# Second normalised rows split by tile and turned by a transposing DMA in the layers of a graph network kernel

## The chip, the cores and the metric

The kernel runs on one core of a Trainium2 chip. The metric is the device time of one execution in microseconds (us), lower is better. Five engines run their own instruction streams and meet only at semaphores: TensorE (PE in the rows), VectorE (DVE), ScalarE (ACT), GpSimd (POOL) and SyncE (SP, which here only issues DMAs). A DMA that SyncE or ScalarE issues stands in the rows as SPq or ACTq.

## The reference

The input is 6250 rows of 512 floats and 100000 edges sorted by destination. One block of a graph transformer is computed:

```
xn = layernorm(x)
x  = x + gnn(xn, src, dst) + linear_attention(xn)
x  = x + mixture_of_experts(layernorm(x))

gnn:  agg = segment_sum(xn[src], dst);  xn @ W1.T + b1 + (agg / deg) @ W2.T + b2
attention: q, k = relu(..), v;  vk = v'k over all rows;  q @ vk, divided by its last column; @ proj.T
experts: scores -> softmax over rows -> pooled row -> gate; best 2 of 8 experts on all rows, gelu twice
```

The rows of the second layernorm are called x2 after the sum and xn2 once normalised. Each expert matmul needs xn2 with features on the partitions, which is why xn2 is turned (transposed) tile by tile.

## The kernel before

**Tiles and stages.** The rows are T = 49 tiles of 128. Stage one normalises the rows, splits each float into a high and a low half in float16 (together near float32), stores them to a table in HBM and turns each tile into `xT[:, t]` (128 partitions x 8 x 128 float16: four high chunks, four low ones). Of the tiles from 21 on, two in three are turned by a transposing DMA from SyncE (18 in all), the others by TensorE. Then come the key products ("the K stage") and a short middle part.

**The layers.** `layer(i)`, i = 1 to 48, runs on every engine in a hand-written order. In layer i TensorE does the query matmuls of tile SEQ[i], turns the mean and the attention row of SEQ[i-1] (`turn_ah`, `turn_p`), multiplies (`own`, `gathered`, `mixed`), adds up neighbour rows for a tile ahead (`add_units`), and as its last work turns xn2 of SEQ[i-2] (`turn_x2`, four float32 transposes into a PSUM bank). SEQ is the order of the tiles, 0 to 37 first; tiles 47 and 48 (LATE) come between and their second half is done after the rest.

**Where the turned rows go.** At the start of layer i ScalarE copies the bank of tile SEQ[i-3] as the high half to `xT` (`x2T_high`), and VectorE subtracts it from the bank for the low half (`x2T_low`). Their place in the queues of ScalarE and VectorE matters: on ScalarE `x2T_high` stands right behind `keep_ah`, which ends the layer before, and ahead of `deviation`, `ahT_high` and `pT_high`; on VectorE `x2T_low` stands ahead of `statistics`, `ahT_low`, `pT_low`, `normal` and the rest. `gathered` on TensorE waits for `ahT_low` of the same layer.

**The gathers.** GpSimd issues 782 indirect DMAs (line 811), one each 128 rows of the table, four to a step. A ring of 16 slots holds four steps, so the gathers of step n+4 may not be issued before TensorE has added step n (`add_step`, line 928). The first is issued in the K stage, the last near the end of the layers. Three steps or so fall in a layer; a table computed at build time (`PLAN`) fixes where in TensorE's queue each is added.

**Spills.** The mean of a tile is made ahead of its use. For tiles below SPILLED = 25 it is written to HBM after `keep_ah` (`spill`, SyncE) and read back later (`fetch`, SyncE). In the loop over the layers SyncE does in this order:

```
if t not in LATE and t + WRITE < SPILLED:
    fetch(t + WRITE)
if AHEAD[i] is not None and AHEAD[i] < SPILLED:
    spill(AHEAD[i])
```

`spill(AHEAD[i])` waits for `keep_ah`, the last thing that ScalarE does in layer i. By the tables of the kernel the layers with a spill are i = 1, 2, 3, 5, 6, 7, 9, 10, 11, 13, 14, 15, 17, 18 and 19.

Of the kernel before, what the change touches and what calls it, by code (L numbers as in the profile page):

```python
# [16 lines left out]
ALU = mybir.AluOpType  # L17
ACT = mybir.ActivationFunctionType
# [3 lines left out]
N, D, E = 6250, 512, 100000  # L22
# [4 lines left out]
T = (N + P - 1) // P  # L27
# [52 lines left out]
def after(eng, sem, count):  # L80

    if not isinstance(count, int) or count > 0:
        eng.wait_ge(sem, count)
# [14 lines left out]
LATE = (T - 2, T - 1)  # L98
SEQ = [*range(38), LATE[0], *range(38, 42), LATE[1], *range(42, T - 2)]
K_AT, K_STEP, M_PARTS, LAYER, GATHERS, LANDING, ADDING, UNITING = 5.0, 5.75, (7.5, 3.5, 8.0), 11.9, 5.02, 5.0, 0.55, 1.6  # L100
TURN = {t: i for i, t in enumerate(SEQ)}
# [3 lines left out]
def by_pe(t):  # L105

    return t < TURNED or t % 3 == 0


def pairs_until(i):  # L110
# [135 lines left out]
def weight_steps():  # L246

    at, i = {}, WEIGHTS_FROM
    for step in WEIGHT_STEPS:
        while i in TILES_K:  # L250
            i += 1
        at[i] = step
        i += 1
    assert i <= T
    return at


STEPS = {**EDGE_STEPS, **weight_steps()}
ORDER = [STEPS[i] for i in sorted(STEPS)]
STEPS_ALL, EDGES_ALL = len(ORDER), len(EDGE_STEPS)  # L260
# [8 lines left out]
def program(nc, x, src, dst, gw1, gb1, gw2, gb2, qkv_w, proj_w, proj_b, attn_w, attn_b, gate_w, gate_b,  # L269
            w1, b1, w2, b2, out):  # L270
    ctx = ExitStack()
    with ctx:
# [9 lines left out]
        xT = sb("xT", [P, T, 2 * C, P], F16)  # L282
# [56 lines left out]
        x2, xn2, acc, pT_, x_in, w32, ahT_ = (work[:, k] for k in range(7))  # L339
# [112 lines left out]
        s = {n: ctx.enter_context(nc.semaphore(n)) for n in names}  # L452
# [37 lines left out]
        def stored(eng, t):  # L490

            if t >= 0:
                eng.wait_ge(row_stored[t % NS], 16 * (t // NS) + 16 * len(parts(P if t < T - 1 else TAIL)))

        def late(t):

            return isinstance(t, int) and t == T - 1
# [17 lines left out]
        def tile(t):  # L515

            return xT[:, bass.ds(t, 1), :, :].rearrange("p t a n -> p (t a) n")
# [13 lines left out]
        def _(sp):  # L531
# [35 lines left out]
            for t in range(XI, T + XI):  # L567
                r = t - XI
                if t < T:
                    n = TAIL if t == T - 1 else P  # L570
# [13 lines left out]
                n = TAIL if r == T - 1 else P  # L584
# [30 lines left out]
            landed = [0]  # L615

            def turn(t):
# [6 lines left out]
                landed[0] += 1  # L624
                sp.dma_start_transpose(xT[:, t, :, :], natural(t)).then_inc(s["tile_landed"], 16)

            def spill(t):

                sp.wait_ge(s["ah_made"], t + 1)
                after(sp, s["mean_stored"], 16 * t)  # L630
                sp.dma_start(spilled[t * P:(t + 1) * P, :], mean_in(t)).then_inc(s["mean_stored"], 16)
# [8 lines left out]
            for i in range(FIRST, T + 2):  # L640
                t = i + 2
# [15 lines left out]
            for i in range(1, T):  # L657
                t = SEQ[i - 1]
                if t not in LATE and t + WRITE < SPILLED:
                    fetch(t + WRITE)  # L660
                if AHEAD[i] is not None and AHEAD[i] < SPILLED:
                    spill(AHEAD[i])

            sp.wait_ge(s["gate_steps"], C + 3)
            chosen = []
# [185 lines left out]
        def _(pe):  # L851
# [311 lines left out]
            def turn_x2(t):  # L1163

                pe.wait_ge(s["xn2_made"], t + 1)
                after(pe, s["x2T_lo"], t - 1 if late(t) else t)
                if late(t):
                    pe.wait_ge(s["ahT_lo"], T)
                for c in range(C):
                    r = nc.tensor.transpose(x2T_bank(t)[:, c * P:(c + 1) * P], xn2_of(t)[:, c * P:(c + 1) * P], ident[:])  # L1170
                r.then_inc(s["turned_x2"], 1)
# [6 lines left out]
            def layer(i):  # L1178

                query(SEQ[i])  # L1180
                steps_at(i, 0)
                t = SEQ[i - 1]
                if t not in LATE:
                    turn_ah(t)
                turn_p(t)
                steps_at(i, 1)
                own(t)
                steps_at(i, 2)
                if t not in LATE:
                    gathered(t)  # L1190
                steps_at(i, 3)
                mixed(t).then_inc(s["lin_made"], 1)
                steps_at(i, 4)
                if AHEAD[i] is not None:
                    add_units(AHEAD[i])
                if i >= 2 and SEQ[i - 2] not in LATE:
                    turn_x2(SEQ[i - 2])
            for i in range(1, T):
                layer(i)
# [95 lines left out]
        def _(act):  # L1295
# [151 lines left out]

            def x2T_high(t):

                act.wait_ge(s["turned_x2"], t + 1)  # L1450
                F(tile(t)[:, 0:C, :], x2T_bank(t)[:, :].rearrange("p (c n) -> p c n", c=C), ACT.Copy).then_inc(s["x2T_hi"], 1)

            def deviation(t):
# [155 lines left out]
        def _(dve):  # L1609
# [411 lines left out]
            def x2T_low(t):  # L2021

                after(dve, s["x2T_hi"], t + 1)
                V.tensor_tensor(tile(t)[:, C:2 * C, :], x2T_bank(t)[:, :].rearrange("p (c n) -> p c n", c=C),
                                tile(t)[:, 0:C, :], ALU.subtract).then_inc(s["x2T_lo"], 1)

# [21 lines left out]
            def normal(t):  # L2048

                k = int(late(t))  # L2050
                after(dve, s["std2_made"], t + 1)
                V.reciprocal(rstd2[:, k], std2[:, k]).then_inc(s["rs2_made"], 1)
                after(dve, s["rs2_made"], t + 1)
                after(dve, s["turned_p"] if late(t) else s["turned_x2"], T if late(t) else t)
                V.tensor_scalar(xn2_of(t), x2_of(t), mv2[:, k, 0:1], rstd2[:, k], ALU.subtract, ALU.mult
                                ).then_inc(s["xn2_made"], 1)

# [288 lines left out]
```

## Time and profile before

| | |
|---|---|
| median of 3 runs | 1464.06 us (1461.55 to 1466.59) |
| the profiled execution, its own time | 1465.09 us |
| its span in the trace | 1462.9 us |
| stage one | to about 150 us |
| gathers issued | 146.8 to 1147.0 us |
| the layers | about 400 to 1150 us |
| experts | from about 1190 us |

Every number read from the trace below is of that one profiled execution, in us from the start of its span unless ns is written. The 2 us between span and own time are start and end of the program and are taken as unchanged.

### The profile page before, as it was taken

The page shows a single profiled execution, that of the slowest core. Times are in us where ns is not written, and L with a number is a line of the kernel's source. Part 1 is how long each engine was busy: PE and PEld are TensorE (multiplying, and loading weights), DVE is VectorE, ACT ScalarE, POOL GpSimd, SP SyncE. Part 2 cuts the span into 40 slices and gives each one's busy share as a digit, 9 for nine tenths or more (in the row PEclk, how much of TensorE's full clock was granted, in tenths as well). Part 3 has the DMA queues.
Part 4 walks back from the last instruction along what each step waited for, and adds up shares of the span by engine and source line. Part 5 has one row for each costly group of instructions (what it writes and reads, how often), then busy time and mean ns, then how long its engine had stood idle before and what let it go on. Part 6 is the DMA issues. An engine that isn't in the chain of part 4 may idle for free.

```text
span 1462.9 us, 22936 instructions
## 1 busy us (share of the span) xinstructions
PE 1372.7 (94%) x7764; PEld 625.1 (43%) x7764; DVE 940.4 (64%) x2087; ACT 610.3 (42%) x938; POOL 834.0 (57%) x907
## 2 busy tenths in 40 slices
PE   7888989999999999999999999899996889999997
PEld 3444434444444444444444444344442344444443
DVE  8877343222566877777777767666764466776677
ACT  5645223232233444444434444333332436555554
POOL 4653777777777777777777777777777200000000
PEclk9999999999999999999999999999998989999998
DMA  6854889998888888888887777877877341223322
GB/s 202 259 184 166 254 224 245 238 253 236 269 276 262 280 273 272 281 270 280 252 247 237 238 250 236 251 239 234 249 239 239 110 145 49 91 90 115 115 86 100
DMA packets 141205, 312.09 MB, mean 213 GB/s; under 512 B 40050, under 2 KB 42636, under 8 KB 141108
## 3 DMA queue, kind: packets, MB, share of 16 engines
q0 software_dynamic: 62560, 205.05, 46.7%
q1 hardware_dynamic: 62608, 77.26, 16.9%
q10 hardware_dynamic: 15940, 28.54, 5.3%
q8 instruction: 56, 0.92, 0.3%
q14 instruction: 41, 0.34, 0.1%
HBM read 260.53 MB, written 45.52 MB: 209 GB/s over the span
## 4 chain that ended last, share of the span: by engine, by line
PE 50%; POOL 25%; issue 10%; DVE 8%; DMA 4%; ACT 2%; SPq 0%; DVEq 0%; ACTq 0%; POOLq 0%
POOL ring L811 24%; PE bank L857 13%; PE bank L858 12%; PE bank L862 12%; PE bank L928 4%; DMA ring<-table,src_col 2%; PE bank L946 1%; PE bank L947 1%; PE bank L1121 1%; PE bank L996 1%; DVE xT L1669 1%; PE bank L997 1%; PE bank L998 1%; DVE st L1659 1%; DVE ring L2290 1%
## 5 line engine op out<-in xcount | busy, mean ns | idle before, releaser
L811 POOL DMA_INDIRECT ring<-table,src_col x782 | 759.6, 971 | 251.1 <-issue 242.7
L857 PE MATMUL bank<-wts,xT 128*128 128x512 f16 x588 | 226.2, 385 | 3.9 <-DVE wts L1875 2.1
L858 PE MATMUL bank<-wts,xT 128*128 128x512 f16 x588 | 226.0, 384 | 0.0
L928 PE MATMUL bank<-ring,hot 128*32 128x512 f16 x1560 | 121.3, 389 | 40.2 <-DMA ring<-table,src_col 32.1
L857 PE MATMUL bank<-wts,work 128*128 128x512 f16 x392 | 152.5, 389 | 1.5 <-ACT work L1463 1.4
L862 PE MATMUL bank<-wts,xT 128*128 128x512 f16 x588 | 152.9, 383 | 0.0
L858 PE MATMUL bank<-wts,work 128*128 128x512 f16 x392 | 151.6, 387 | 0.0
L1351 ACT ACTIVATE work<-bank,rd 128x512 f32<-128x512 f32 x49 | 33.7, 687 | 187.4 <-DVE rd L1832 186.3
L1899 DVE TENSOR_TENSOR work<-work 128x512 f16<-128x512 f32 x32 | 22.3, 696 | 137.6 <-ACT work L1409 137.4
L862 PE MATMUL bank<-wts,work 128*128 128x512 f16 x392 | 101.1, 380 | 0.0
L1593 ACT ACTIVATE work<-work 128x512 f32<-128x512 f32 x98 | 61.8, 630 | 79.9 <-DVE work L2300 78.8
L857 PEld LDWEIGHTS bank<-wts,xT 128*128 128x128 f16 x588 | 57.9, 98 | 76.9 <-issue 21.4
L862 PEld LDWEIGHTS bank<-wts,xT 128*128 128x128 f16 x588 | 58.2, 99 | 71.6 <-issue 4.0
L1778 DVE SCALAR_TENSOR_TENSOR units<-bank,units 128x512 f16<-128x512 f32 x65 | 44.7, 688 | 66.3 <-ACT units L1342 65.6
L1342 ACT ACTIVATE units<-bank 128x512 f16<-128x512 f32 x65 | 38.6, 595 | 116.6 <-PE bank L928 110.6
L858 PEld LDWEIGHTS bank<-wts,xT 128*128 128x128 f16 x588 | 58.1, 99 | 55.2 <-issue 2.2
L2300 DVE SCALAR_TENSOR_TENSOR work<-bank,mix,work 128x512 f32<-128x512 f32 x98 | 69.9, 746 | 15.0 <-PE bank L862 9.8
L2290 DVE SCALAR_TENSOR_TENSOR ring<-work,gexp,ring 128x512 f32 (+1 forms) x98 | 73.3, 748 | 9.2 <-DVE ring L2290 4.1
L857 PE MATMUL bank<-xT,wts 128*128 (+2 forms) x208 | 75.0, 367 | 2.9 <-ACT wts L1571 2.9
L1406 ACT ACTIVATE work<-bank 128x512 f32<-128x512 f32 x49 | 29.1, 594 | 112.3 <-PE bank L862 112.3
L858 PE MATMUL bank<-xT,wts 128*128 (+2 forms) x208 | 75.0, 367 | 0.0
L857 PE MATMUL bank<-wts,ring 128*128 128x512 f16 x196 | 74.3, 379 | 0.0
(307 smaller groups left out, 2523.8 us busy)
## 6 DMA issues: line engine op xcount, KB each, us to landing
x_rows<-work ACTq DMA_DIRECT2D x51, 256.0 KB
ring<-table,src_col POOLq DMA_INDIRECT x782
work<-in_x ACTq DMA_DIRECT2D x48, 256.0 KB
ring<-x_rows SPq DMA_DIRECT2D x12, 1024.0 KB, 5.1
out_x<-ring SPq DMA_DIRECT2D x12, 1024.0 KB
table<-xT SPq DMA_DIRECT2D x45, 256.0 KB, 3.2
ring<-in_x SPq DMA_DIRECT2D x44, 256.0 KB, 3.3
spilled<-work SPq DMA_DIRECT2D x25, 256.0 KB, 3.8
```

What stands on the lines that cost most here:

```text
L811: pool.indirect_dma_start(ring[:, k, :], None, table[:, :], bass.IndirectOffsetOnAxis(ap=ap, axis=0)).then_inc(sem, 16)
L857: mm(out_, wh(c), mh(c), start=first and c == 0, stop=False)
L858: mm(out_, wh(c), ml(c), start=False, stop=False)
L862: r = mm(out_, wl(c), mh(c), start=False, stop=last and c == n - 1)
L928: r = mm(ps_unit[a:a + WIDE, :], hot[:, u % 2, DEEP * j + k, :], ring[:, slot(n, j), h * D:(h + 1) * D], start=(k == 0 and h == 0), stop=( ...
L1342: F(units[:, u % HOLD, 0:D], ps_unit[:, :], ACT.Copy, scale=SU).then_inc(s["unit_hi"], 1)
L1351: F(mean_in(t), agg_bank(t)[:, :], ACT.Copy, scale=rd_of(t)).then_inc(s["ah_made"], 1)
L1406: F(k32, k_bank(i)[:, :], ACT.Relu, scale=SK).then_inc(s["k32_made"], 1)
L1593: F(act2[:, j % 2, e], pre[:, j % 2, e], ACT.Gelu).then_inc(s["act_made"], 1)
L1778: V.scalar_tensor_tensor(out=units[:, u % HOLD, D:2 * D], in0=ps_unit[:, :], scalar=SU, in1=units[:, u % HOLD, 0:D], op0=ALU.mult, op1=ALU ...
L2290: r = V.scalar_tensor_tensor(out=y, in0=act2[:, j % 2, e], scalar=gexp[:, e:e + 1], in1=y, op0=ALU.mult, op1=ALU.add)
L2300: V.scalar_tensor_tensor(out=pre[:, j % 2, e], in0=bank[4 + 2 * (j % 2) + e][:, :], scalar=mix[:, 4:5], in1=b2b[:, e], op0=ALU.mult, op1=A ...
```

## The change

For tiles 0 to 43 (below X2_PE = 44) TensorE no longer turns xn2. ScalarE now copies xn2 itself, from SBUF and not turned, as float16 into the slot of the next tile in `xT`, which is free once `own` of that tile has been done; VectorE puts the low half beside it; and SyncE turns both halves at once by a transposing DMA into the tile's own slot. Tiles 44 to 48 are turned as before.

```
+X2_PE = T - 5
+LANDED = sum(not by_pe(t) for t in range(T))
...
+        def x2_rows(t):
+            return xT[:, SEQ[TURN[t] + 1]].rearrange("p a n -> p (a n)")
...
 SyncE
+            def turn_x2(t):
+                sp.wait_ge(s["x2T_hi"], t + 1)
+                sp.wait_ge(s["x2T_lo"], t + 1)
+                sp.wait_ge(s["tile_landed"], 16 * landed[0])
+                landed[0] += 1
+                sp.dma_start_transpose(xT[:, t, :, :], x2_rows(t)).then_inc(s["tile_landed"], 16)
...
                 if AHEAD[i] is not None and AHEAD[i] < SPILLED:
                     spill(AHEAD[i])
+                if i >= 3 and SEQ[i - 3] < X2_PE:
+                    turn_x2(SEQ[i - 3])
...
 TensorE
+                if t == X2_PE:
+                    pe.wait_ge(s["tile_landed"], landed + 16 * X2_PE)
...
-                if i >= 2 and SEQ[i - 2] not in LATE:
+                if i >= 2 and X2_PE <= SEQ[i - 2] < LATE[0]:
                     turn_x2(SEQ[i - 2])
...
 ScalarE
             def x2T_high(t):
-                act.wait_ge(s["turned_x2"], t + 1)
+                if t < X2_PE:
+                    act.wait_ge(s["xn2_made"], t + 1)
+                    act.wait_ge(s["lin_made"], TURN[t] + 2)
+                    after(act, s["tile_landed"], 16 * (LANDED + t))
+                    F(x2_rows(t)[:, 0:D], xn2, ACT.Copy).then_inc(s["x2T_hi"], 1)
+                    return
+                act.wait_ge(s["turned_x2"], t + 1 - X2_PE)
...
 VectorE
             def x2T_low(t):
                 after(dve, s["x2T_hi"], t + 1)
+                if t < X2_PE:
+                    V.tensor_tensor(x2_rows(t)[:, D:2 * D], xn2, x2_rows(t)[:, 0:D], ALU.subtract
+                                    ).then_inc(s["x2T_lo"], 1)
+                    return
```

`normal` on VectorE, which overwrites xn2, waited for `turned_x2` and now waits for `x2T_lo` of the tile before.

SyncE's queue in the layers, before, around the spills of layers 5 and 6. L638 is `fetch`, L631 is `spill`; the brackets name the semaphores waited for.

```order
L638 DMA work<-spilled 128x512 [waits mean_loaded,turned_ah,mean_stored] x2
L631 DMA spilled<-work 128x512 [waits mean_stored,ah_made]
L638 DMA work<-spilled 128x512 [waits mean_loaded,turned_ah,mean_stored]
L631 DMA spilled<-work 128x512 [waits mean_stored,ah_made]
L638 DMA work<-spilled 128x512 [waits mean_loaded,turned_ah,mean_stored]
L631 DMA spilled<-work 128x512 [waits mean_stored,ah_made]
```

The same place in the changed kernel, where L654 is `fetch`, L647 `spill` and L641 `turn_x2` on SyncE.

```order
L654 DMA work<-spilled 128x512 [waits mean_loaded,turned_ah,mean_stored]
L641 DMA_TRANSPOSE xT<-xT 128x8x128 [waits tile_landed,x2T_lo,x2T_hi]
L654 DMA work<-spilled 128x512 [waits mean_loaded,turned_ah,mean_stored]
L647 DMA spilled<-work 128x512 [waits mean_stored,ah_made]
L641 DMA_TRANSPOSE xT<-xT 128x8x128 [waits tile_landed,x2T_lo,x2T_hi]
L654 DMA work<-spilled 128x512 [waits mean_loaded,turned_ah,mean_stored]
L647 DMA spilled<-work 128x512 [waits mean_stored,ah_made]
L641 DMA_TRANSPOSE xT<-xT 128x8x128 [waits tile_landed,x2T_lo,x2T_hi]
```

In a layer with a spill the transposing DMA now stands behind the spill; in one without it stands behind the fetch alone.

ScalarE's queue over the seam of two layers, before. L1492 loads a row of x, L1351 is `keep_ah`, L1451 is `x2T_high`, L1458 is `deviation`, L1463 and L1468 are `ahT_high` and `pT_high`.

```order
L1492 DMA work<-in_x 128x512 [waits x_loaded2,sraw_made]
L1351 ACTIVATE work<-bank,rd 128x512 [waits mean_stored,rd_made]
L1451 ACTIVATE xT<-bank 128x512 [waits turned_x2]
L1458 ACT_TABLE_LOAD [waits rs2_made]
L1458 ACTIVATE std<-mv,epsc 128x1 [waits mv2_made]
L1463 ACTIVATE work<-bank 128x512 [waits turned_ah]
L1468 ACTIVATE work<-bank 128x512 [waits turned_p]
```

The same place in the changed kernel, where L1474 is `x2T_high`.

```order
L1518 DMA work<-in_x 128x512 [waits x_loaded2,sraw_made]
L1371 ACTIVATE work<-bank,rd 128x512 [waits mean_stored,rd_made]
L1474 ACTIVATE xT<-work 128x512 [waits tile_landed,lin_made,xn2_made]
L1484 ACT_TABLE_LOAD [waits rs2_made]
L1484 ACTIVATE std<-mv,epsc 128x1 [waits mv2_made]
L1489 ACTIVATE work<-bank 128x512 [waits turned_ah]
L1494 ACTIVATE work<-bank 128x512 [waits turned_p]
```

No instruction moved on ScalarE; the wait of one is another: `tile_landed`, the landing of the transposing DMA of the tile before.

## Rows read from the trace of the kernel before

**Rows 1.** The page: engines, and the chain that ended last.

```profile
PE 1372.7 (94%) x7764; PEld 625.1 (43%) x7764; DVE 940.4 (64%) x2087; ACT 610.3 (42%) x938; POOL 834.0 (57%) x907
PE 50%; POOL 25%; issue 10%; DVE 8%; DMA 4%; ACT 2%; SPq 0%; DVEq 0%; ACTq 0%; POOLq 0%
```

**Rows 2.** The gathers alone (line 811): durations in ns, then GpSimd's idle time before them.

```profile
L811 POOL DMA_INDIRECT ring<-table,src_col x782: 942/946/2807, 146.8 to 1147.0; - x196
...
  issue: 242.7, 766
  PE bank L928: 8.4, 16
```

**Rows 3.** Windows: length, PE, PEld, DVE, ACT, POOL busy; clock, DMA share, GB/s.

```profile
250.00:300.00 50.00, 48.76 (x300) 21.57 (x298) 14.15 (x30) 16.98 (x28) 37.98 (x40) 1.00 0.93 240
...
550.00:600.00 50.00, 50.00 (x304) 23.00 (x303) 38.28 (x93) 23.09 (x36) 38.05 (x40) 1.00 0.86 274
```

**Rows 4.** Timeline of TensorE in layer 7: start, length, line, operation.

```profile
488.15 0.60 PE L1170 MATMUL bank<-ident,work 128*128 128x128 f32 x4
488.58 0.38 PE L857 MATMUL bank<-wts,xT 128*128 128x512 f16 x1
...
495.97 0.39 PE L857 MATMUL bank<-wts,work 128*128 128x512 f16 x1
...
501.25 0.61 PE L928 MATMUL bank<-ring,hot 128*32 128x512 f16 x8
```

**Rows 5.** Timeline of SyncE's queue at the same seam.

```profile
489.45 0.32 SPq L631 DMA_DIRECT2D spilled<-work  x1
```

**Rows 6.** Timeline of ScalarE at the same seam.

```profile
488.74 0.69 ACT L1351 ACTIVATE work<-bank,rd 128x512 f32<-128x512 f32 x1 [4.65 <-DVE rd L1832]
489.32 0.59 ACT L1451 ACTIVATE xT<-bank 128x512 f16<-128x512 f32 x1
```

**Rows 7.** Timeline of VectorE in layer 7.

```profile
490.95 0.68 DVE L2024 TENSOR_TENSOR xT<-bank,xT 128x512 f16<-128x512 f32 x1
...
493.40 0.69 DVE L2038 TENSOR_TENSOR work<-bank,work 128x512 f16<-128x512 f32 x1 [0.84 <-ACT work L1463]
...
499.09 0.68 DVE L1778 SCALAR_TENSOR_TENSOR units<-bank,units 128x512 f16<-128x512 f32 x1
```

**Rows 8.** Transposing DMAs (line 625): all, then that issued at 227.8 alone.

```profile
L625 SPq DMA_TRANSPOSE xT<-xT x16: 1232/1236/1367, 159.6 to 322.1; - x16
...
DMA to landing us min/median/max: 3.4/5.3/7.6
...
DMA to landing us min/median/max: 7.6/7.6/7.6
```

**Rows 9.** The transposing DMA at 322.1 alone, and DMA issues of the page.

```profile
DMA to landing us min/median/max: 5.4/5.4/5.4
...
spilled<-work SPq DMA_DIRECT2D x25, 256.0 KB, 3.8
```

**Rows 10.** TensorE around a wait of 3.90 us, and windows of its granted clock.

```profile
948.84 0.62 PE L928 MATMUL bank<-ring,hot 128*32 128x512 f16 x8 [3.90 <-DMA ring<-table,src_col]
...
949.40:952.60 3.20, 3.20 (x12) 1.17 (x9) 1.16 (x2) 0.60 (x1) 2.59 (x3) 0.50 0.76 214
953.00:956.00 3.00, 3.00 (x17) 1.62 (x16) 0.42 (x3) 0.06 (x1) 2.39 (x3) 1.00 0.71 217
```

**Rows 11.** A gather, the VectorE instruction beside it, and that one's group on the page.

```profile
298.00 1.44 POOL L811 DMA_INDIRECT ring<-table,src_col  x1 [0.30 <-issue]
...
297.93 0.69 DVE L1899 TENSOR_TENSOR work<-work 128x512 f16<-128x512 f32 x1 [6.39 <-ACT work L1409]
...
L1899 DVE TENSOR_TENSOR work<-work 128x512 f16<-128x512 f32 x32 | 22.3, 696 | 137.6 <-ACT work L1409 137.4
```

**Rows 12.** TensorE adds step 105; GpSimd issues the first gather of step 109.

```profile
696.70 0.61 PE L928 MATMUL bank<-ring,hot 128*32 128x512 f16 x8
...
706.63 0.95 POOL L811 DMA_INDIRECT ring<-table,src_col  x1 [0.30 <-issue]
```

More of the change, by code:

```diff
@@ L2053, in normal @@
                 after(dve, s["rs2_made"], t + 1)
-                after(dve, s["turned_p"] if late(t) else s["turned_x2"], T if late(t) else t)
+                if late(t):
+                    dve.wait_ge(s["turned_p"], T)
+                elif t > X2_PE:
+                    dve.wait_ge(s["turned_x2"], t - X2_PE)
+                else:
+                    after(dve, s["x2T_lo"], t)
                 V.tensor_scalar(xn2_of(t), x2_of(t), mv2[:, k, 0:1], rstd2[:, k], ALU.subtract, ALU.mult
```

## Prediction

> **What bounds the kernel now.** I read the page first. TensorE is busy 94% of the span and the chain that ended last lies half on it [rows 1], which invites the thought that every matmul taken away shortens the time. The next view contradicts that. The gathers run from 146.8 to 1147.0 us, 782 of them. One takes 0.95 us of GpSimd, and nearly all the idle time before them is "issue", 242.7 us in 766 pieces or 0.3 us each; TensorE is named as releaser in 16 places with 8.4 us together, and most of those are the usual 0.3 us too [rows 2]. So one gather goes out every 1.25 us, 782 x 1.25 = 978 of the 1000 us, and GpSimd hardly ever waits. The windows show how close TensorE runs beside it: from 550 to 600 us it is busy the full 50 us while GpSimd issues its 40 gathers [rows 3]. The layers are thus bound by the gather stream, with TensorE level with it. The ring of four steps is the buffer between the two: step 105 is added by 697.3 us, and the gathers of step 109 begin at 706.6 [rows 12], so TensorE could be about 9 us later there before GpSimd had to stop. TensorE earlier is worth nothing; TensorE later is free up to 9 us and then costs time that is not won back, since after it GpSimd still needs 1.25 us for each gather.
>
> **What is removed.** Four float32 transposes a tile. They begin at 488.15 and the next layer's first matmul at 488.58 [rows 4]: 0.43 us each time, 44 x 0.43 = 19 us of TensorE. By the paragraph above that by itself brings about 0.
>
> **What is moved.** The copy on ScalarE reads SBUF and not PSUM; I keep the 0.59 us of the old one [rows 6], since size and output are the same. VectorE's low half takes 0.68 us now [rows 7], and the same form from SBUF takes 0.70 on average [rows 11]. Both at nothing. `normal` waits for an earlier instruction of its own engine: nothing.
>
> **What is added: a wait of ScalarE for a DMA that stands behind a spill.** This is the term that decides. `x2T_high` of a tile now waits until the transposing DMA of the tile before has landed. In a layer without a spill that DMA can be issued as soon as its low half is made, early in the layer: the low half ends at 491.63 in the sample layer [rows 7], 12 us before the next seam, and landing takes 3.4 to 7.6 us [rows 8]. Hidden. In a layer with a spill SyncE's queue holds it behind `spill`, and that waits for `keep_ah`, ScalarE's last work of the layer. The very next instruction of ScalarE is the one that needs the landing. Nothing can hide it.
>
> The seam of layers 6 and 7, step by step. `keep_ah` ends at 489.43 [rows 6]. The spill is issued at 489.45 and takes 0.32 [rows 5], so the transposing DMA goes out at 489.8. Its landing takes 5.3 us in the median of 18 [rows 8]; four of them were issued about 2 us behind a spill and took 7.6, 5.7, 6.5 and 5.4 (first and last in [rows 8, 9]), median 6.1, and here the spill is even closer. I take 6.1: it lands at 495.9. ScalarE's copy ends near 496.5, and VectorE's low half starts there and not at 490.95 [rows 7]: 5.6 us late. On VectorE everything behind it in the layer is late by as much. `ahT_low` would end at 494.09 + 5.6 = 499.7, and `gathered` on TensorE wants it at 495.97 [rows 4, 7]: TensorE waits 3.7 us. The low half of the unit that ended, 499.77 + 5.6 = 505.4, is wanted for the next step at 501.25 [rows 4, 7]: 4.1 us, so little more than the first wait.
>
> A wait of 3.7 us also costs clock. After TensorE's wait of 3.90 us the granted clock is 0.50 in the window from 949.4 to 952.6, the level of 1.2 GHz, and 1.00 again from 953; 12 matmuls are begun there in 3.2 us where 17 go in 3.0 after it [rows 10]. Half of 3.4 us is 1.7 us lost. Ten of the eleven waits of 2 us or more in this trace are followed by such a drop, so I book 1.5. One seam then costs TensorE 3.7 + 1.5 = 5.2 us.
>
> How many: layers with a spill from 3 on (before that no tile is turned) are 3, 5, 6, 7, 9, 10, 11, 13, 14, 15, 17, 18 and 19, thirteen. 13 x 5.2 = 68 us, less 0.43 x 18 = 8 us that TensorE has saved in layers 3 to 20, is 60 us by which TensorE is later at the end of layer 20. The ring gives about 9 [rows 12]: GpSimd loses 51. From layer 21 the order is harmless, TensorE is 0.43 us a layer quicker, and the gather stream sets the pace again, 51 us later.
>
> **A smaller added cost: VectorE in GpSimd's way.** The gather at 298.00 took 1.44 us and not 0.95, and VectorE's subtraction with both inputs in SBUF ran from 297.93 to 298.62 beside it [rows 11]. Over the 32 instructions of that line the excess of overlapping gathers comes to 3.9 us, 0.12 each; over the 49 old low halves, with one input in PSUM, to nothing. The new low half has the form of the first. It counts only where gathers set the pace, in some 24 layers after the spills: 24 x 0.12 = 3 us. Bounds: 0 (it never straddles a gather's start) and 24 x 0.5 = 12 (it always does, at the 0.5 of that row). I take 3.
>
> The Trainium skill, page SBUF — State Buffer, section "Who interferes with whom", has VectorE instructions with two SBUF inputs contend with a GpSimd instruction that reads SBUF, and adds that a probe saw no `tensor_tensor` stall a DMA; by its latter half this term would be 0. The row speaks for the first half.
>
> **The sum.** 51 + 3 = 54 us on the profiled execution's own 1465.1 us is 1519; against the median of the runs, 1 us lower, **1518 us**.
>
> The Trainium skill, page Advanced Engine Details and Errata, section "X-Bar Transpose (TRN2)", says transposing DMAs are as fast as regular ones. A plain spill of the same size lands in 3.8 us [rows 9] against the 5.3 of [rows 8]; by the page a seam would cost 2.3 us less and the sum would be 1488. The rows disagree with it, and I follow them.
>
> **The rivals.**
> *The wait is hidden (no change, or a shade slower).* If the transposing DMA were issued before the spill, or ScalarE had slack at the seam, only the 19 us of idle TensorE and the contention remain: 1464 + 0 to 44 x 0.12 = 1464 to 1469. For it: ScalarE is busy 42% [rows 1]. Against it: the queue orders of SyncE and ScalarE as printed, and VectorE and `gathered`, which leave only 495.97 - 494.09 = 1.9 us.
> *Faster.* If the chain's 50% on TensorE were the truth and GpSimd were the one held back, all 19 us would come out: 1445. It decides if GpSimd's gap before gathers in the layers shrinks below 0.3 us; the 766 equal gaps speak against it [rows 2].
> *The DMA engines fill up.* Their share is 0.86 in the layers with spills, and 0.93 in the K stage with transposing DMAs under way, where GpSimd still issues 40 gathers in 50 us [rows 3, 8]. If the added ones pushed the need to 1.05 of what the engines do over 300 us, gathers would be late by 15 us with no seam wait: 1479. It decides from a share of 1.0 on.
>
> **How the numbers follow.** Seam wait as forecast 0.82; hidden 0.07 (same 0.05, slower 0.02); DMA engines full without it 0.05; faster 0.06. A change under 0.3% (4.4 us) can't be told from none here. Slower is 0.82 + 0.02 + 0.05 = 0.89, same 0.05, faster 0.06. Within the forecast: landing at 4.5 us and no clock loss makes a seam 2.1 (or 2.5 by the unit's wait), 13 x 2.5 - 17 + 3 = +19; landing at 4.5 with the clock loss 3.6, +33; landing at 7.6 with it in full 6.9, 13 x 6.9 - 17 + 3 = +76. The range leaves out the other cases (0.18 together) and only the very ends of this one: 1485 to 1541.
>
> **What would show it.** Right: ScalarE idle about 6 us ahead of L1474, released by the DMA into xT, thirteen times and not in layers 5, 9, 13, 17 or after 20; TensorE waiting 3 to 4 us ahead of `gathered` in the next layer with the clock at 0.5 behind it; those layers near 20 us long and not 15; GpSimd released by TensorE (L928) for some 50 us between 450 and 750; the last gather near 1200; the experts unchanged. Wrong: the transposing DMA issued well before `keep_ah` ends in spill layers, landings under 4 us, or GpSimd's gaps still at 0.3 us throughout. If the last gather comes at 1147 and the time is 1464, the wait was hidden; if it comes earlier, the bound was misread.

## The result and the profile after

The changed kernel takes 1537.57 us in the median of its runs (1535.23 to 1540.5) and the kernel before 1465.32 us on the same chip: 1.0508 times as long, 95% interval 1.0484 to 1.0531; the medians lie 72 us apart. The forecast was 1518 (1485 to 1541). The profiled execution's own time is 1535.6 us, its span 1533.4, against 1465.1 of before: 70.5 us more.

The page of the kernel after: the engines' busy time, then the shares of the chain that ended last, by engine and by line. They answer to [rows 1].

```profile
PE 1374.7 (90%) x7588; PEld 608.0 (40%) x7588; DVE 941.5 (61%) x2087; ACT 611.8 (40%) x938; POOL 837.1 (55%) x907
...
PE 47%; POOL 18%; DVE 12%; DMA 10%; issue 8%; ACT 3%; SPq 0%; ACTq 0%; DVEq 0%; POOLq 0%
```

TensorE has 176 matmuls fewer and is busy 2 us longer. 19 us of work have gone, so about 21 have come in, and they are not work: the matmuls at half clock are longer. DMA was 4% of the chain and is 10%.

The waits of the kernel after: engine, line, what ended the wait; us in total, times, longest. The last row but one is that of the matmuls behind `gathered`'s wait; the line numbers are about 20 above those of before (gathers L829, `x2T_high` L1474, its low half L2051, `ahT_low` L2068, `add_step` L946).

```profile
ACT xT L1474 <- DMA xT<-xT: 86.3, 13, 9.0
POOL ring L829 <- PE bank L946: 83.0, 37, 9.7
DVE xT L2051 <- ACT xT L1474: 76.0, 13, 8.2
PE bank L875 <- DVE work L2068: 55.7, 13, 6.7
PE bank L946 <- DMA ring<-table,src_col: 36.4, 18, 4.5
```

Read from the top this is the predicted chain: ScalarE waits 13 times for the landing, VectorE waits 13 times for ScalarE, TensorE 13 times for VectorE, and GpSimd, which was released by TensorE for 8.4 us in [rows 2], for 83.0. The seam between layers 6 and 7, which the prediction worked through, one queue at a time (start, length; in brackets the idle time before and what ended it):

```profile
506.57 0.32 SPq L647 DMA_DIRECT2D spilled<-work  x1
506.99 1.37 SPq L641 DMA_TRANSPOSE xT<-xT  x1
```

```profile
505.86 0.69 ACT L1371 ACTIVATE work<-bank,rd 128x512 f32<-128x512 f32 x1 [6.90 <-DVE rd L1858]
513.45 0.63 ACT L1474 ACTIVATE xT<-work 128x512 f16<-128x512 f32 x1 [6.91 <-DMA xT<-xT]
...
514.11 0.69 DVE L2051 TENSOR_TENSOR xT<-work,xT 128x512 f16<-128x512 f32 x1 [5.96 <-ACT xT L1474]
...
517.33 0.39 PE L875 MATMUL bank<-wts,work 128*128 128x512 f16 x1 [4.61 <-DVE work L2068]
```

`keep_ah` (L1371) ends, the spill and then the transposing DMA go out at once, and 6.5 us after its issue ScalarE's copy starts, which in [rows 6] followed `keep_ah` without a gap. Windows of the kernel after, with the columns of [rows 3]: 3.2 us around the end of the wait of layer 4 (TensorE starts again at 457.5), then the stretch that answers to the second window of [rows 3].

```profile
456.70:459.90 3.20, 2.38 (x6) 0.89 (x7) 2.99 (x9) 2.30 (x4) 2.59 (x3) 0.50 1.19 243
...
550.00:600.00 50.00, 39.71 (x208) 16.29 (x207) 27.72 (x70) 17.02 (x26) 31.50 (x33) 0.90 0.83 236
```

The granted clock is at 0.50, the level of 1.2 GHz, when TensorE starts again and behind it; and in 50 us GpSimd issues 33 gathers and no longer 40.

The gathers' line of the page, after:

```profile
L829 POOL DMA_INDIRECT ring<-table,src_col x782 | 762.9, 976 | 319.0 <-issue 236.0
```

Before, they ran from 146.8 to 1147.0 us; now from 146.2 to 1217.8. The same gather lies 0.6 us later than before at 442 us, 67.5 later at 830, and the last one 70.8 later. The experts behind them take 316 us in both.

### The profile page after: what moved, and what is told of

It is laid out like the page before. It is cut to its first block, busy times and chain, and to the rows that moved or that the text cites. A ratio compares the mean times of both kernels' runs of the same rounds, so it can differ in the third digit from the quotient of the medians.

```text
span 1533.4 us, 22673 instructions
## 1 busy us (share of the span) xinstructions
PE 1374.7 (90%) x7588; PEld 608.0 (40%) x7588; DVE 941.5 (61%) x2087; ACT 611.8 (40%) x938; POOL 837.1 (55%) x907
## 3 DMA queue, kind: packets, MB, share of 16 engines
q1 hardware_dynamic: 109072, 88.80, 22.4%
## 4 chain that ended last, share of the span: by engine, by line
PE 47%; POOL 18%; DVE 12%; DMA 10%; issue 8%; ACT 3%; SPq 0%; ACTq 0%; DVEq 0%; POOLq 0%
POOL ring L829 17%; PE bank L875 12%; PE bank L876 12%; PE bank L880 11%; DMA xT<-xT 5%; PE bank L946 3%; DMA ring<-table,src_col 2%; PE bank L964 2%; PE bank L965 1%; DMA work<-in_x 1%; PE bank L1014 1%; PE bank L1015 1%; PE bank L1016 1%; DVE st L2060 1%; DVE xT L2051 1%
## 5 line engine op out<-in xcount | busy, mean ns | idle before, releaser
L829 POOL DMA_INDIRECT ring<-table,src_col x782 | 762.9, 976 | 319.0 <-issue 236.0
L875 PE MATMUL bank<-wts,work 128*128 128x512 f16 x392 | 160.1, 408 | 57.1 <-DVE work L2068 55.7
L946 PE MATMUL bank<-ring,hot 128*32 128x512 f16 x1560 | 122.5, 392 | 49.4 <-DMA ring<-table,src_col 36.4
L876 PE MATMUL bank<-wts,work 128*128 128x512 f16 x392 | 159.7, 407 | 0.0
L1371 ACT ACTIVATE work<-bank,rd 128x512 f32<-128x512 f32 x49 | 33.6, 687 | 194.1 <-DVE rd L1858 194.1
L880 PE MATMUL bank<-wts,work 128*128 128x512 f16 x392 | 107.5, 399 | 0.0
L875 PEld LDWEIGHTS bank<-wts,work 128*128 128x128 f16 x392 | 40.1, 102 | 132.2 <-DVE work L2068 64.4
L2325 DVE SCALAR_TENSOR_TENSOR ring<-work,gexp,ring 128x512 f32 (+1 forms) x98 | 73.2, 747 | 9.2 <-DVE ring L2325 4.1
L2051 DVE TENSOR_TENSOR xT<-work,xT 128x512 f16<-128x512 f32 x44 | 30.4, 691 | 76.0 <-ACT xT L1474 76.0
```

What stands on the lines that cost most here:

```text
L829: pool.indirect_dma_start(ring[:, k, :], None, table[:, :], bass.IndirectOffsetOnAxis(ap=ap, axis=0)).then_inc(sem, 16)
L875: mm(out_, wh(c), mh(c), start=first and c == 0, stop=False)
L876: mm(out_, wh(c), ml(c), start=False, stop=False)
L880: r = mm(out_, wl(c), mh(c), start=False, stop=last and c == n - 1)
L946: r = mm(ps_unit[a:a + WIDE, :], hot[:, u % 2, DEEP * j + k, :], ring[:, slot(n, j), h * D:(h + 1) * D], start=(k == 0 and h == 0), stop=( ...
L1371: F(mean_in(t), agg_bank(t)[:, :], ACT.Copy, scale=rd_of(t)).then_inc(s["ah_made"], 1)
```

## The experiments

Each was run on the chip with its own profile; "before" is the kernel before on the same chip (medians 1464.4 to 1466.0). The edits are shown in excerpts; waits and lines that follow from them are left out. Everything read from a trace is of one execution.

**1. The transposing DMA ahead of the spill.**

```diff
+                if i >= 3 and SEQ[i - 3] < X2_PE:
+                    turn_x2(SEQ[i - 3])
                 if AHEAD[i] is not None and AHEAD[i] < SPILLED:
                     spill(AHEAD[i])
-                if i >= 3 and SEQ[i - 3] < X2_PE:
-                    turn_x2(SEQ[i - 3])
```

Expected: 

> The change with one edit: SyncE issues the transposing DMA of the second rows ahead of the spill of the same layer, not behind it. Everything else, TensorE's missing transposes and VectorE's low half from SBUF included, stays. Theory of the seam wait: the DMA needs only the two halves, which are made early in the layer, so it lands before the next seam, ScalarE's 13 idle gaps ahead of L1474 are gone, the spill layers are 15 us long again, and what stays is the contention of the low half with gathers: 1465 + 3, 1465 to 1470 us. Rival, the added transposing traffic itself (DMA engines full, slower transposition): the traffic is the same as in the change, so most of the 72 us stays, 1500 us or more. Rival, TensorE bound the layers: 19 us fewer of TensorE come out, near 1446 us.

Measured: 1472.07 us, 1.0053 of before (1.0034 to 1.0071). Two lines in another order take back 65 of the 72 us. The traffic is the same, TensorE's work is the same; what is gone is the wait. ScalarE waits for no transposing DMA at all: L1474 has 24.6 us of waits for TensorE and 2.5 for a store, none for `xT<-xT`. What stays, 6 us by the medians and 7 on the profiled execution, is more than the 3 that were expected; 1472 lies 2 us above the expected range. It shows in the gathers, whose busy time was 759.6 us before:

```profile
L829 POOL DMA_INDIRECT ring<-table,src_col x782 | 765.3, 979 | 252.0 <-issue 241.0
```

From the first to the last gather it is 1006.1 us against 1000.1 before: 5.7 of the 6.0 are the longer gathers.

**2. The same, with TensorE transposing too.**

```diff
-                if i >= 2 and X2_PE <= SEQ[i - 2] < LATE[0]:
+                if i >= 2 and SEQ[i - 2] not in LATE:
                     turn_x2(SEQ[i - 2])
```

Expected: 

> The first experiment with TensorE doing its four transposes of the second rows for all tiles again, into a PSUM tile that nobody reads; the copies still come from SBUF and the DMA still does the real transposing. So TensorE has its 44 x 0.43 = 19 us back as pure extra work, and VectorE's acc waits for it as before. Theory (the gather stream bounds the layers and TensorE's saved time is worth nothing): within 2 us of the first experiment. Rival (TensorE bound): 19 us above it. In between, if TensorE's ring of four steps was nearly empty: some 5 us.

Measured: 1478.74 us, 1.0091 (1.0065 to 1.0118), 6.7 above the first. Neither theory, but nearest to the in-between case: of the 19 us of extra TensorE about a third comes through. The six runs lie in two groups, 1474 to 1476 and 1482 to 1485 us; the trace is of one of the second group. In it VectorE's sum of x2 waits for the input rows, and TensorE for it. The same row of experiment 1 stands first for comparison:

```profile
DVE work L2041 <- DMA work<-in_x: 14.4, 10, 3.3
```

```profile
DVE work L2041 <- DMA work<-in_x: 38.9, 15, 6.9
```

```profile
650.36 0.75 DVE L2041 SCALAR_TENSOR_TENSOR work<-bank,mix,work 128x512 f32<-128x512 f32 x1 [6.87 <-DMA work<-in_x]
...
651.95 0.61 PE L875 MATMUL bank<-wts,xT 128*128 128x512 f16 x1 [4.25 <-DVE work L2044]
```

These are the row of the waits in experiments 1 and 2, then VectorE and TensorE in time in experiment 2. The wait was 7.8 us in 4 places before. Where the rows land late, the DMA engines are full. The windows from 540 to 640 us of before, of experiment 1 and of experiment 2 (each fence one kernel):

```profile
540.00:640.00 100.00, 100.00 (x607) 45.70 (x604) 75.34 (x184) 45.68 (x69) 75.93 (x80) 1.00 0.86 274
```

```profile
540.00:640.00 100.00, 96.21 (x569) 41.48 (x567) 73.77 (x183) 44.15 (x65) 76.40 (x78) 1.00 0.99 292
```

```profile
540.00:640.00 100.00, 94.88 (x567) 42.22 (x565) 70.30 (x175) 41.74 (x63) 75.62 (x79) 1.00 1.01 282
```

The last column but one is the share of the 16 DMA engines: 0.86, 0.99, 1.01. The likely reading, which no run tests by itself: with such late landings TensorE loses time, and then each 0.43 us that it has too much keeps it from catching up. Why the landings of experiment 2 are later than those of experiment 1, whose transfers are the same, stays open.

**3. The normalised rows in the freed PSUM bank** (on top of 1).

```diff
         def xn2_of(t):
+            if t < X2_PE:
+                return bank[0][:, :]
```

Expected: 

> The first experiment with the normalised second rows of the 44 tiles kept in the PSUM bank that the change has freed, instead of in SBUF, so that VectorE's raw score, normalisation and low half have one input in PSUM and no longer two in SBUF. Theory of contention: gathers beside an instruction with two SBUF inputs take up to 1.4 us and not 0.95, 0.05 to 0.12 us for each such instruction; with those gone GpSimd's gathers are 6 to 10 us shorter in all, and since the gather stream bounds the layers the time falls by as much: 1455 to 1461 us, under the kernel before. Rival (overlap is chance, or VectorE's SBUF inputs don't matter to GpSimd): the same as the first experiment within 1 us, or slower if the PSUM operand makes VectorE's instructions longer.

ScalarE's copy now waits for the pooled sum of its tile, the last reader of the rows. Measured: 1465.0 us, 0.9997 (0.998 to 1.0014), 7 us under the first, but 4 us above the expected 1461. The gathers' line of its page, and VectorE at one place in time:

```profile
L831 POOL DMA_INDIRECT ring<-table,src_col x782 | 756.5, 967 | 254.4 <-issue 242.4
```

```profile
581.12 0.75 DVE L2043 SCALAR_TENSOR_TENSOR work<-bank,mix,work 128x512 f32<-128x512 f32 x1 [2.37 <-DMA work<-in_x]
```

The gathers are 8.8 us shorter than in the first, as the theory of contention wants, although `normal`, with its output in PSUM, takes 0.81 us and not 0.55. It doesn't beat the kernel before, 3.1 us of shorter gathers notwithstanding: GpSimd waits 3.6 us more for TensorE (12.0 against 8.4), in places where the input rows landed late, as in the second row.

**4. The change as it was, with the clock kept up in the wait.**

```diff
                 steps_at(i, 2)
+                if i - 1 in SEAMS:
+                    warm(14, ps_tx)
                 if t not in LATE:
                     gathered(t)
```

Expected: 

> The change as it is, with 14 matmuls of no use added on TensorE ahead of the gathered sum in each of the 13 layers that follow a spill, where TensorE waits about 4.3 us. They fill the wait and keep the granted clock up; the wait of ScalarE for the transposing DMA stays. Theory: 10 of the 13 seams show the clock at 0.50 behind the wait, 47.8 us in all, half of it lost, 24 us; with the clock kept at 1.00 the time is 15 to 24 us under the change, 1514 to 1523 us. Rival (the lost clock is hidden in the ring, only the wait for the DMA counts): within 4 us of the change, 1534 to 1540. If the added matmuls outlast the wait, some of the gain is given back.

Measured: 1523.09 us, 1.0404 (1.0374 to 1.0433), 14.5 us less than the change, at the lower end of the expected gain. Work of no use on TensorE makes the kernel faster. ScalarE's 13 waits are untouched, 87.0 us:

```profile
ACT xT L1477 <- DMA xT<-xT: 87.0, 13, 8.4
POOL ring L830 <- PE bank L947: 66.0, 32, 7.0
```

The clock is down for 13.7 us in layers 4 to 20, at four seams, and not for 44.4 at ten. (The 47.8 of the expectation holds 3.4 more, from layer 23, which is no seam.) So the cost of a seam is in two parts, the wait and the clock behind it, and the second is real: half of the 30.7 us is 15.

**5. The input rows loaded earlier** (on top of 3).

```diff
                 early = t is not None and t < X2_PE
+                if early:
+                    load_x(SEQ[i - 1], x, None, entry(t) + 1)
                 if t is not None and t not in LATE:
                     score(t)
```

Expected: 

> The third experiment, with the load of the next tile's input rows issued earlier: the raw score's discarded product goes into the SBUF slot that the normalised rows have left, so the slot of the input rows is free once x2 is summed, and ScalarE issues its load ahead of score(t) and not behind it, about 3.5 us earlier. In the third experiment VectorE waited 25.9 us in 11 places for that load, and GpSimd ran into TensorE at 598, 614, 821 and 836 us, 4.6 us over its usual gaps. Theory: with the DMA engines nearly full the load lands late, and these waits are all of what the freed bank didn't bring; they go, and the time is 4 to 6 us under the third experiment, 1459 to 1461 us, under the kernel before by more than 0.3%. Rival (the run-outs come from TensorE's own load): the same as the third experiment within 2 us.

The raw score's product now goes to the slot of the normalised rows. Measured: 1475.81 us (1464.72 to 1492.86), 1.005 (1.0024 to 1.0076), by the medians 11 us above the third. It was expected to be faster. Three of the eleven runs lie at 1465 to 1466 us, as the third experiment, and seven at 1475 to 1480; the profiled one, 1479.7, is the slowest of the seven, so what follows is the slow case. VectorE's waits for the load are gone, and others have come in their place: GpSimd waits 32.6 us for TensorE. Two rows of its waits, then one transposing DMA on SyncE's queue and the copy on ScalarE that waited for it, then the window in which it was under way:

```profile
ACT xT L1476 <- DMA xT<-xT: 21.6, 4, 7.4
DVE work L2050 <- DMA x_rows<-work: 19.1, 3, 7.4
```

```profile
623.81 1.64 SPq L643 DMA_TRANSPOSE xT<-xT  x1
...
637.88 0.60 ACT L1476 ACTIVATE xT<-bank 128x512 f16<-128x512 f32 x1 [7.37 <-DMA xT<-xT]
```

```profile
620.00:640.00 20.00, 16.07 (x99) 6.98 (x98) 10.62 (x24) 7.93 (x12) 15.23 (x16) 0.98 1.09 253
```

One transposing DMA took 14 us from its issue to the copy that waited for it. The reading that fits, though no run tests it alone: with the DMA share at 1.0 and above an earlier load only chooses whose transfer is late, here the store of x2 and the transposing one. The expectation's claim that the load's waits are all that stood in the way is refuted. Why this order is in most runs worse than the third's, and in three not, was not settled.

**6. The saving alone: three of four transposes left out of the kernel before.**

```diff
-                for c in range(C):
+                for c in range(1 if 0 < t < T - 5 else C):
```

Expected: 

> The kernel before, with TensorE doing only the first of the four transposes of the second rows for 43 tiles (three quarters of those rows are left out of the computation: the copies read old data). Nothing else is changed, so this is the change's saving alone, 43 x 0.32 = 14 us of TensorE, with no DMA added. Theory (the gather stream bounds the layers): nothing, 1463 to 1467 us. Rival (TensorE bounds): 14 us less, 1451. A part of it, 1 to 3 us, may come out in the layers ahead of the gathers' steady stretch and behind the last gather.

Measured: 1466.58 us, 1.001 (0.9996 to 1.0024). 14 us of TensorE's matmuls are worth nothing: from 400 to 1130 us its idle time grows from 29.6 to 43.1 us, by just as much. The gathers run from 145.1 to 1144.8, 999.7 us (before 1000.1). In the kernel before, the gather stream sets the pace.

**7. The wait alone, in the kernel before.**

```diff
                     spill(AHEAD[i])
+                    if i >= 3:
+                        sp.dma_start(means[i * P:(i + 1) * P, :], xT[:, SEQ[i] + 1].rearrange("p a n -> p (a n)")
+                                     ).then_inc(s["slow_lists"], 16)
...
             def x2T_high(t):
+                after(act, s["slow_lists"], 16 * sum(i in SEAMS for i in range(t + 3)))
```

Expected: 

> The kernel before, with the wait alone: behind each of the 13 spills from layer 3 on SyncE issues a plain DMA of 256 KB from an xT slot to a DRAM tensor that nobody reads, and ScalarE's copy of the transposed rows in the next layer waits for it. TensorE still transposes. Theory of the seam wait: a plain DMA lands in 3.8 to 4.5 us, so ScalarE waits about 4.8 us at a seam and not 6.6; TensorE waits some 2.3 us and in part loses 1.7 of clock; 13 x 2.3 to 4 less 6 of the ring is 24 to 46 us: 1489 to 1511 us. Rival (it is not the wait but the transposing DMA's traffic or the lost transposes that cost the time): 1466 within 3 us.

Measured: 1505.06 us, 1.0268 (1.0241 to 1.0296): 40 us more from 13 plain DMAs and the wait for them, with TensorE transposing as ever, and within the expected 1489 to 1511. The landing of the added DMAs, then the waits:

```profile
DMA to landing us min/median/max: 3.9/4.1/6.2
```

```profile
ACT xT L1456 <- DMA means<-xT: 64.4, 13, 6.6
...
PE bank L861 <- DVE work L2043: 28.2, 15, 3.8
```

It has the same links as the change, each a size smaller: 5.0 us a seam on ScalarE (6.6 in the change), 2 us on TensorE (4.3).

**8. The change with a plain DMA in place of the transposing one.**

```diff
-                sp.dma_start_transpose(xT[:, t, :, :], x2_rows(t)).then_inc(s["tile_landed"], 16)
+                sp.dma_start(xT[:, t].rearrange("p a n -> p (a n)"), x2_rows(t)).then_inc(s["tile_landed"], 16)
```

Expected: 

> The change with a plain DMA of the same 256 KB in place of the transposing one, in the same place of the queue (the second rows arrive unturned, so the values behind them are others). Theory by the traces' landings (plain 3.8 us, transposing 5.3, 6.2 at the seams): it lands about 2 us earlier at each of the 13 seams, TensorE waits 2 us less and loses its clock less often: 26 to 33 us less than the change, 1504 to 1512 us. Rival (transposing DMAs are as fast as plain ones, the landing is that of the queue and of the gathers' traffic): the same as the change within 5 us.

Measured: 1512.85 us, 1.0319 (1.029 to 1.0349), 24.7 us less than the change, a little less than the expected 26 to 33.

```profile
ACT xT L1474 <- DMA xT<-xT: 71.5, 13, 7.3
```

ScalarE waits 5.5 us a seam and no longer 6.6, TensorE 41.7 us in all and no longer 55.7, and while TensorE works the clock is down for 24.1 us and not 39.5. 14.0 us less of waits and half of 15.4 make 21.7; the two profiled executions lie 20.6 us apart. The wait stays, and so do two thirds of the loss: that the DMA turns the rows makes the wait longer by a fifth, and is not what makes it.

**9. The change in tiles 18 to 43 only**, those turned behind the last spill.

```diff
+        def by_dma(t):
+            return X2_FROM <= t < X2_PE
...
-                if i >= 3 and SEQ[i - 3] < X2_PE:
+                if i >= 3 and by_dma(SEQ[i - 3]):
                     turn_x2(SEQ[i - 3])
```

Expected: 

> The change in 26 of its 44 tiles only: the second rows of tiles 18 to 43, which are turned in layers 21 and later, go by the transposing DMA, in the change's own order on SyncE; those of tiles 0 to 17 are turned by TensorE as before. No transposing DMA stands behind a spill any more and the DMA engines have room (share 0.79 before in 840 to 930 us). Theory (the loss is the wait at seams with a spill; a full set of DMA engines, share 0.97 to 1.0, is the next bound in the layers with spills): no seam waits, no run-outs, only the contention of the low half with gathers, 26 x 0.12 = 3 us: 1466 to 1469. Rival (transposing DMAs cost wherever they stand, 26/44 of 72 us): above 1490.

Measured: 1464.3 us, 1.0012 (1.0 to 1.0025), no difference that this measurement tells. 26 transposing DMAs cost next to nothing where no spill stands ahead of them. The 3 us that were expected for the low halves did not show in the time: the gathers' busy time is 0.9 us above before.

**10. The same, with those rows in the PSUM bank.**

```diff
-            if t < X2_PE:
+            if by_dma(t):
                 return bank[0][:, :]
```

Expected: 

> The ninth experiment with the normalised second rows of tiles 18 to 43 kept in the PSUM bank that TensorE's transposes leave free there, as in the third. Theory: in the third experiment the gathers took 756.5 us and not 765.3 as in the first, but the run-outs of the layers with spills gave 4.6 us back, where DMA engines were full; here those layers are as before, and in the rest the gathers are 26/44 of 8.8 = 5 us shorter than in the ninth, 2 to 3 shorter than before: 1461 to 1464, under the kernel before by 0 to 0.3%. Rival (the shorter gathers don't reach the end, since TensorE sets the pace of the late layers): 1466, as before.

SyncE's order is that of the first experiment, which changes nothing here, since no spill comes after layer 19. Measured: 1461.41 us, 0.9986 (0.9969 to 1.0003): 2 us under before as the ratio has it, 3 by the medians, as expected in size, but the interval reaches 1. The gathers' lines of experiments 9 and 10:

```profile
L834 POOL DMA_INDIRECT ring<-table,src_col x782 | 760.5, 973 | 253.1 <-issue 244.6
```

```profile
L836 POOL DMA_INDIRECT ring<-table,src_col x782 | 755.3, 966 | 251.1 <-issue 243.9
```

The PSUM bank makes the gathers 5.2 us shorter over 26 tiles here, 8.8 over 44 in experiment 3: 0.20 us a tile both times.

## Why the prediction was right, step by step

**What bounds the kernel before**: the gather stream, with TensorE's saving worth about 0. Right: experiment 6 takes 14 us from TensorE and changes nothing.

**The wait of ScalarE behind the spill**: right in kind and number. It was forecast 13 times at 6.5 us and came 13 times with 86.3 us, 6.6 each. The 13 landings, from issue to the copy, were 4.1 to 8.5 us with a mean of 6.2; 6.1 was taken. Experiment 1 removes the wait by order alone and takes back 65 of 72 us; experiment 7 makes it in the kernel before and loses 40.

**TensorE's wait**: 3.7 forecast, 55.7/13 = 4.3 measured. This is a term mis-sized. The prediction let TensorE save 0.43 us in each of the layers and took 8 us off the loss. At a seam it can't be saved: TensorE, without its four transposes, comes to `gathered` 0.43 us sooner and waits so much longer. 3.7 + 0.43 = 4.1 is nearly the measured figure; 13 x 0.43 = 5.6 of the 8 us were thus counted twice. All of TensorE's idle time from 400 us to the end of layer 20 grew by 58.1 us (61.2 against 3.1), where the forecast had 13 x 3.7 = 48.1.

**The clock**: 13 x 1.5 = 19.5 forecast; the granted clock stood at 0.50 for 44.4 us in layers 4 to 20, at ten of the 13 seams (the three without a drop are the three shortest waits, 2.25, 2.19 and 2.82 us). 4.9 us of it fall into the waits themselves, in layers 4, 6 and 10, where the clock is already down when TensorE starts again; half of the other 39.5 is 19.7 lost, as forecast. Experiment 4 shows that it counts: 14.5 us came back with the clock. Together 58.1 + 19.7 less 0.43 x 18 = 7.7 is 70.1, and layer 21 begins at 764.1 us and not at 694.0, 70.1 later. The forecast had 60. (Of the waits of 2 us or more in the kernel before, the trace has twelve behind the first matmul, eleven of them with a drop, and not ten of eleven.)

**The ring**: 9 forecast, read at step 105, and there it gave just that. It is not the step that counts in the end. In the table the margin is the time in the kernel before from the end of adding a step to the first gather that needs its slots; the others say how much later the adding and that gather are in the change:

| step | margin before | TensorE later by | gathers later by |
|---|---|---|---|
| 105 | 9.3 | 70.1 | 61.0 |
| 110 | 6.2 | 70.0 | 64.0 |
| 112 | 7.8 | 75.0 | 67.4 |
| 128 | 5.4 | 73.2 | 68.0 |

A gather that has waited starts 0.3 us behind the step, so what is passed on is TensorE's delay less the margin, plus 0.3. Over the layers the margins before go from 5.4 to 12 us, and each delay meets the small ones. TensorE's own delay also grew behind the last seam, where the prediction called the order harmless: in layer 23 VectorE waits for its input rows and TensorE for VectorE.

```profile
796.45 0.75 DVE L2041 SCALAR_TENSOR_TENSOR work<-bank,mix,work 128x512 f32<-128x512 f32 x1 [2.59 <-DMA work<-in_x]
...
801.20 1.04 PE L946 MATMUL bank<-ring,hot 128*32 128x512 f16 x8 [4.48 <-DVE units L1804]
```

The same wait of TensorE was 1.1 us in the kernel before, and here the clock is at 0.50 for 3.4 us behind it: 4.9 us more. The share of the DMA engines from 780 to 795 us is 0.97. So the ring gave 7.6 us, not 9, where the gathers' delay reached 67.4, and 70.1 had become 75.0.

**VectorE in GpSimd's way**: 3 forecast, 0.12 a low half, and the trace bears it out. Gathers that overlap one of the 44 new low halves are together 4.1 us longer than their median of 0.946 us would make them, 2.9 of it in the 26 after layer 21 begins; one took 1.42 us. In experiment 1 it is 6.5 us, in experiment 9, with 26 of them, 3.4. With one input in PSUM it is 0.0 in the kernel before (49 low halves), 0.2 in experiment 3 (44) and 0.0 in experiment 10 (26). The other readers of the rows go the same way from experiment 1 to 3, the raw score from 1.7 to 0.1 us and the pooled sum from 4.7 to 2.1; a gather beside two instructions counts for both. The total of all gathers says less: it is 3.3 us higher in the change, but 3.2 higher in experiment 7 too, which has no new low half, and 5.2 higher in experiment 4 than in the change, with the same VectorE. By the Trainium skill, page SBUF — State Buffer, section "Who interferes with whom", an instruction of VectorE with two SBUF inputs contends with one of GpSimd that reads SBUF, but no `tensor_tensor` stalled a DMA in a probe. The traces agree with the first. They don't bear out a term of 0, which the prediction drew from the second: the low half is a `tensor_tensor`, and the gathers beside it are longer.

**Landing**: plain against transposing. The Trainium skill, page Advanced Engine Details and Errata, section "X-Bar Transpose (TRN2)", has them equally fast. In experiment 8, with all else the same, the plain one lets ScalarE go 1.1 us a seam sooner and the kernel is 24.7 us faster; the rows disagree with the page, though by less than the 2.3 us that the prediction took from [rows 8, 9].

**The rivals**: "hidden" was refuted by the 13 waits, "faster" by experiment 6. "The DMA engines fill up" had the right limit and the wrong place. In the change itself TensorE's waits keep the demand down (share 0.83 from 550 to 600 us). When the seam wait is taken out, as in experiments 1, 2, 3 and 5, the share goes to 0.97 to 1.03 from 440 to 640 us, and landings get late. The traces point to it as the next bound behind the one that was removed, in experiments 2, 3 and 5 above all. Experiment 9, which adds its DMAs only behind those layers, is 8 us faster than experiment 1 by the medians, 6 by the ratios; no run varies the share alone.

Sum: of the 70.5 us on the profiled execution the forecast had 54. Of the 16.5 missing, 10 are TensorE's waits up to layer 20 (5.6 of them counted twice as a saving), 5 its wait in layer 23 with the clock behind it, and 1.5 the ring's. The gathers' delay grew from there by 3.4 us to the last, forecast 3. The mechanism and the number of seams were right; the time came out inside the range although the sum was a quarter short.

## What to carry to other kernels

When a transfer is moved to a queue, look first at what stands ahead of it there and what that waits for: here an independent spill, whose source was the last work of the layer, held back a DMA whose own inputs had been ready some 11 us earlier (experiment 1 issues one at 481.2 us where `keep_ah` ends at 492.6), and two lines in another order were worth 65 us. Work taken off an engine that then waits is no saving, and mustn't be subtracted from the wait. Before putting more transfers beside a stream of gathers, read the share of the DMA engines in the busiest layers: from 0.86 there was room for less than was added.

## What the runs showed of the hardware

- A transposing DMA of 256 KB took more of the DMA engines than a plain one. SyncE's queue on the page of the change (packets, MB, share of 16 engines over the span), then on that of experiment 8, where 44 of them are plain:

```profile
q1 hardware_dynamic: 109072, 88.80, 22.4%
```

```profile
q1 hardware_dynamic: 68944, 88.80, 18.8%
```

  The bytes are the same. 22.4% of 1533.4 us is 343 us, 18.8% of 1512.0 is 284: 59 us over 44 DMAs, 1.3 us of all 16 engines more for each.
- In a stretch with a share of 1.09 one transposing DMA took 14 us until its waiter started (experiment 5), where the 13 of the change that ScalarE waited for at a seam took 4.1 to 8.5.
- With 14 matmuls of no use in a wait of TensorE the granted clock stayed at 1.00 at nine of 13 seams and not at three, and the kernel was 14.5 us faster (experiment 4).
- Gathers beside a subtraction of VectorE with both inputs in SBUF were 4.1 us longer over 44 of them (6.5 in experiment 1), and with one input in PSUM 0.0 to 0.2. With the normalised rows in PSUM for all their readers the gathers got shorter by 0.20 us a tile (experiments 3 and 10).
